# Residual and score carried in the gathered row: the second mixture's tiles scatter finished rows into the output

## What is computed

```python
def _L1_ffn_ref(hidden_states, w_red, wg, W1, b1, W2, b2):
    B, T, E, C, H, G = (2, 512, 8, 256, 512, 16)
    x = hidden_states.reshape(-1, c)
    x_red = x @ w_red
    wg_n = wg / jnp.maximum(jnp.linalg.norm(wg, axis=1, keepdims=True), 0.0001)
    logits = x_red @ wg_n.T
    gates = jax.nn.softmax(logits, axis=1)
    scores = jnp.max(gates, axis=1)
    idx = jnp.argmax(gates, axis=1)
    h = gelu(x @ W1[idx] + b1[idx])          # the expert that idx names
    o = h @ W2[idx] + b2[idx]
    o = o * scores[:, None]
x = x + _L1_ffn_ref(_layernorm(x, axis=-1), ...)
```

## Time and profile before

| | |
|---|---|
| median of 3 runs | 1151.25 us (1150.07 to 1156.2) |
| span of the profiled execution | 1143.9 us, first to last instruction |
| that execution's own time | not shown apart; the median is 7.35 us above its span |
| busy share of PE, DVE, ACT, POOL | 86%, 65%, 42%, 25% |
| last attention stage and routing | 912 to 1039 us |
| second mixture | 1039 to 1128 us |
| after it | 1128 to 1143.9 us |

### The profile page before, as it was taken

The page is one execution under the profiler, slowest core; times in us unless marked ns, Lnnn a source line. Parts: engine busy times, 40 slices in busy tenths (PEclk is TensorE's granted clock), DMA queues, the critical chain, the costliest instruction groups (busy, mean ns, idle before and its releaser), DMA issues.

```text
span 1143.9 us, 20648 instructions
## 1 busy us (share of the span) xinstructions
PE 982.2 (86%) x6905; PEld 591.4 (52%) x6905; DVE 742.5 (65%) x1952; ACT 478.9 (42%) x1055; POOL 280.5 (25%) x242
## 2 busy tenths in 40 slices
PE   7878789878898799999998876898899898987893
PEld 3555455546465488888885442333333333335662
DVE  3484677684878766666663476578777857545665
ACT  3443725342433344444442320446666657532331
POOL 0333524523320233444331001100010011112551
PEclk8999989998998899999999997669999988677997
DMA  8442020003535411111115486233163041231225
GB/s 289 150 129 110 2 74 1 19 1 93 142 98 166 146 49 53 49 53 48 48 40 164 96 152 126 54 42 53 43 112 75 2 131 61 87 126 37 79 76 176
DMA packets 69506, 98.64 MB, mean 86 GB/s; under 512 B 6528, under 2 KB 56960, under 8 KB 66976
## 3 DMA queue, kind: packets, MB, share of 16 engines
q1 hardware_dynamic: 60000, 63.75, 20.3%
q0 software_dynamic: 9408, 33.56, 11.0%
HBM read 70.10 MB, written 27.13 MB: 85 GB/s over the span
## 4 chain that ended last, share of the span: by engine, by line
PE 50%; DVE 28%; ACT 7%; DMA 7%; issue 4%; POOL 2%; SPq 1%; DVEq 0%; ACTq 0%; POOLq 0%
PE pb L1004 11%; PE pb L1021 7%; DVE MX L1943 5%; PE pb L1109 4%; PE pb L1022 3%; PE pb L769 3%; PE pb L1133 2%; PE pb L1087 2%; PE pb L848 2%; PE pb L838 2%; PE pb L792 2%; DMA xr<-rows,gi 2%; PE pb L1057 2%; ACT EX L1423 2%; DVE TQ L1552 1%
## 5 line engine op out<-in xcount | busy, mean ns | idle before, releaser
L1366 ACT ACTIVATE m<-pb,b1m 128x128 f32<-128x128 f32 x404 | 115.5, 369 | 172.0 <-PE pb L1004 169.8
L1423 ACT ACTIVATE EX<-pb 128x512 f32<-128x512 f32 x256 | 137.1, 599 | 115.7 <-PE pb L1133 114.9
L1943 DVE TENSOR_REDUCE MX<-pb 128x1 f32<-128x512 f32 x256 | 158.4, 683 | 41.0 <-PE pb L1087 40.8
L1004 PE MATMUL pb<-xt,w1h 128*128 128x128 f16 x1616 | 157.2, 221 | 3.8 <-issue 3.0
L1021 PE MATMUL pb<-w,mh 128*128 x404 | 149.4, 379 | 5.6 <-DVE ml L1854 5.2
L763 PE MATMUL pb<-identh 128*128 128x512 f16 x558 | 139.9, 408 | 15.5 <-DVE UZ L1588 8.8
L1004 PEld LDWEIGHTS pb<-xt,w1h 128*128 x1616 | 120.4, 99 | 42.0 <-issue 6.0
L1004 PE MATMUL pb<-xt,w1l 128*128 128x128 f16 x808 | 112.5, 220 | 0.0
L1022 PE MATMUL pb<-w,ml 128*128 x404 | 110.1, 273 | 0.0
L2155 POOL DMA_INDIRECT outs<-ob,di x62 | 61.3, 989 | 174.2 <-DVE ob L1869 174.2
L763 PEld LDWEIGHTS pb<-identh 128*128 128x128 f16 x558 | 55.9, 103 | 88.8 <-issue 21.4
(11 more groups left out here) (319 smaller groups left out, 1602.9 us busy)
## 6 DMA issues: line engine op xcount, KB each, us to landing
SR<-in_w1m SPq DMA_DIRECT2D x20, 512.0 KB, 5.6
SR<-in_w2m SPq DMA_DIRECT2D x14, 512.0 KB, 4.5
GB<-outs SPq DMA_DIRECT2D x12, 512.0 KB, 6.8
KS<-kd SPq DMA_DIRECT2D x48, 128.0 KB, 5.6
SRW<-in_w2m SPq DMA_DIRECT2D x10, 512.0 KB, 5.1
QS<-qd POOLq DMA_DIRECT2D x18, 256.0 KB, 10.1
kd<-KHL POOLq DMA_DIRECT2D x8, 512.0 KB, 5.7
vd<-VAB POOLq DMA_DIRECT2D x4, 1024.0 KB, 4.9
```

Source lines behind the costliest of these rows:

```text
L1004: ins = pe.matmul(k.ap[:, h4 * TOK:(h4 + 1) * TOK], wt[:, bass.ds(regs[j], 128)], M.xt[j % 2][:, xc, :], start=i == 0, stop=i == 5)
L1366: ins = act.activation(M.m32[x % 2][:, h4, :], k.ap[:, h4 * TOK:(h4 + 1) * TOK], M.func, bias=M.b1[:, bass.ds(reg + 4 * g + h4, 1)], scale ...
L1423: act.activation(EX[m % len(EX)][:, i, :], k.ap, ACT.Exp, scale=0.25).then_inc(k.out, 1)
L1943: v.tensor_reduce(mx[:, t, 2 * s + j:2 * s + j + 1], k.ap, AX.X, ALU.max).then_inc(k.out, 1)
```

## The change

A row of `rows1` becomes 2,056 bytes: the 1,024 bytes of the two float16 halves, then 256 float32 of the residual `X`, then the score and one zero. In each `gate(b)` SP writes the residual part when `XQ` is done, and the score part when DVE has made `scr` of this batch; for that the exponential of the gate values moves from the routing into each gate, on DVE (subtract, then reduce and reciprocal after `place`) and ACT (exponential). POOL's first gather waits for these writes also. In `experts(E1)` there are seven buffers `xr` in place of four, in the space that `GB1` had; the gather no longer waits for PE's transposes of the buffer's last tile. DVE makes a third operation on each `ob`: times the score plus the residual, both from `xr`. POOL scatters `ob` into the output itself, with a bounds check that leaves out slots whose target is beyond row 2,047. `finish` waits for the last three scatters only.

```diff
-                self.xr = [rings(f"xr{L}_{i}", 128, 2 * D, dt=F16) for i in range(4)]
+                width, dt = ((2 * D, F16), (2 * D + 2, F32))[L]
+                self.xr = [(rings, rest)[L](f"xr{L}_{i}", 128, width, dt=dt) for i in range((4, XR)[L])]
...
-                self.rows = nc.dram_tensor(f"rows{L}", (NT * P, 2 * D), F16, kind="Internal").ap()
-                self.outs = nc.dram_tensor(f"outs{L}", (2 * NT * P + n * TOK, D), F32, kind="Internal").ap()
+                self.rows = nc.dram_tensor(f"rows{L}", (NT * P, width), dt, kind="Internal").ap()
+                self.outs = (nc.dram_tensor("outs0", (2 * NT * P + n * TOK, D), F32, kind="Internal").ap() if L == 0
+                             else out.rearrange("b s d -> (b s) d"))
...
             def gate(b):
+                rows = E1.rows[b * S:b * S + S].rearrange("(t p) d -> p t d", p=128)
                 yield from pause(GAP)
+                w.wait_ge(sem("xg"), b + 1)
+                load("hx", rows[:, :, D:2 * D], X[:, 4 * b:4 * b + 4, :])
                 for n in (GAP, GAP, GAP + 1):
                     M.skip(1)
                     yield from pause(n)
...
                 for _ in range(2):
                     M.skip(1)
                     yield from pause(GAP)
+                w.wait_ge(sem("scr"), b + 1)
+                load("hs", rows[:, :, 2 * D:2 * D + 2], scr[:, 4 * b:4 * b + 4, :])
...
             def finish():
                 all_out(w, E1)
-                for b in range(NB):
-                    load(f"g{b}", GB1[b][:, :, :], E1.outs[b * S:b * S + S].rearrange("(t p) d -> p t d", p=128))
-                for t in range(3, NT, 4):
-                    w.wait_ge(sem("x4"), t // 4 + 1)
-                    load("out", ov[:, t - 3:t + 1, :], X[:, t - 3:t + 1, :])
-                w.wait_ge(sem("d_out"), n["out"])
...
+                w.wait_ge(sem("exz"), b + 1)
+                z = exz[:, 4 * b:4 * b + 4, :]
+                act.activation(z, z, ACT.Exp).then_inc(sem("ez"), 1)
...
+                    if L:
+                        x = M.xr[j % XR]
+                        w.wait_ge(*k.ev)
+                        w.wait_ge(*tile_dma("x", L, j))
+                        v.scalar_tensor_tensor(out=M.ob[j % 3][:, :], in0=M.ob[j % 3][:, :], scalar=x[:, 2 * D:2 * D + 1], in1=x[:, D:2 * D],
+                                               op0=ALU.mult, op1=ALU.add).then_inc(*c.up("done"))
...
                 place(R1, b, psum_m)
+                w.wait_ge(sem("ez"), b + 1)
+                v.tensor_reduce(scr[:, bt, 0], exz[:, bt, :], AX.X, ALU.add).then_inc(*c.up("v"))
+                w.wait_ge(*c.last)
+                v.reciprocal(scr[:, bt, 0], scr[:, bt, 0]).then_inc(*c.up("scr"))
...
                 def fetch(j):
-                    if j >= 4:
+                    if L == 0 and j >= 4:
                         w.wait_ge(*eX.take().mm)
...
                 def store(j):
-                    w.wait_ge(*eD.take().ev)
-                    pool.indirect_dma_start(out=M.outs, out_offset=bass.IndirectOffsetOnAxis(ap=r.di[:, j:j + 1].bitcast(U32), axis=0),
-                                            in_=M.ob[j % 3][:, :], in_offset=None).then_inc(tile_dma("o", L, j)[0], 16)
+                    w.wait_ge(*eD.take().ev if L == 0 else (sem("done"), j + 1))
+                    out_rows = bass.IndirectOffsetOnAxis(ap=r.di[:, j:j + 1].bitcast(U32), axis=0)
...
+                        pool.indirect_dma_start(out=M.outs, out_offset=out_rows, in_=M.ob[j % 3][:, :], in_offset=None,
+                                                bounds_check=NT * P - 1, oob_is_err=False).then_inc(tile_dma("o", L, j)[0], 16)
...
                 w.wait_ge(sem(f"d_hl{L}"), 16 * NB)
+                if L:
+                    w.wait_ge(sem("d_hx"), 16 * NB)
+                    w.wait_ge(sem("d_hs"), 16 * NB)
```

More of the change, by code:

```diff
@@ L237, in build, with __init__ @@
         class Experts:
-            def __init__(self, L, starts, hc, n, func, b1, b2, te, rings):
+            def __init__(self, L, starts, hc, n, func, b1, b2, te, rings, rest=None):
                 self.L, self.hc, self.n, self.func, self.b1, self.b2, self.te = L, hc, n, func, b1, b2, te
@@ L333, in build @@
         lgz1, top1, idxu1 = BZ("lgz1", 128, NT, E), BZ("top1", 128, NT, 8), BZ("idxu1", 128, NT, 8)
-        scr = BZ("scr", 128, NT)
+        scr = BZ("scr", 128, NT, 2)
         tei1 = [BZ(f"tei1_{i}", 1, N1) for i in range(3)]
@@ L348, in build @@
         b2m1 = EZ1("b2m1", 128, E * D)
-        E1 = Experts(1, [[o, o + 8 * K] for o in (MZ.start + 32 * K, MZ.start + 48 * K)] + [[MZ.start + 64 * K, last_zone]], 4, N1, ACT.Gelu, b1m1, b2m1, tei1, EZ1)
-        GB1 = [nc.alloc_sbuf_tensor_at(f"GB1_{i}", [128, 4, D], F32, offset=MZ.start + 4 * i * K) for i in range(NB)]
+        E1 = Experts(1, [[o, o + 8 * K] for o in (MZ.start + 32 * K, MZ.start + 48 * K)] + [[MZ.start + 64 * K, last_zone]], 4, N1, ACT.Gelu, b1m1, b2m1, tei1, EZ1,
+                     Zone(nc, MZ.start, 16 * K))
         PB = [ctx.enter_context(nc.psum_tensor(f"pb{i}", [128, 1024], F32)) for i in range(4)]
@@ L421, in tile_dma @@
         def tile_dma(what, L, j):
-            k = 4 if what == "x" else 3
-            return sem(f"d_e{what}{j % k}"), 16 * (j // k + 1 + (0, (N0 + k - 1 - j % k) // k)[L])
+            k = (4, XR)[L] if what == "x" else 3
+            return sem(f"d_e{what}{L}{j % k}"), 16 * (j // k + 1)
         def all_out(w, M):
@@ L1344, in route @@
                     act.activation(d01[:, :], d01[:, :], ACT.Exp).then_inc(sem("e01"), 1)
-                else:
-                    w.wait_ge(sem("exz"), 1)
-                    act.activation(exz[:, :, :], exz[:, :, :], ACT.Exp).then_inc(sem("ez"), 1)
             def experts(M):
@@ L1828, in route @@
                     v.tensor_tensor(ww[:, 1, :], d01[:, :], ww[:, 0, :], ALU.mult).then_inc(*c.up("ww"))
-                else:
-                    v.tensor_tensor(exz[:, :, :], lgz1[:, :, :], top1[:, :, 0:1].to_broadcast([128, NT, E]), ALU.subtract).then_inc(*c.up("exz"))
-                    w.wait_ge(sem("ez"), 1)
-                    v.tensor_reduce(scr[:, :], exz[:, :, :], AX.X, ALU.add).then_inc(*c.up("v"))
-                    w.wait_ge(*c.last)
-                    v.reciprocal(scr[:, :], scr[:, :]).then_inc(*c.up("scr"))
             def experts(M):
@@ L1993, in wg_norm @@
                 v.memset(R1.Mc[:, :], 0.0)
+                v.memset(scr[:, :, :], 0.0)
                 w.wait_ge(sem("d_we"), 3 * 16)
@@ L2033, in gate @@
                 w.wait_ge(*c.last)
+                bt = slice(4 * b, 4 * b + 4)
+                v.tensor_tensor(exz[:, bt, :], lgz1[:, bt, :], top1[:, bt, 0:1].to_broadcast([128, 4, E]), ALU.subtract).then_inc(*c.up("exz"))
                 for t in range(4 * b, 4 * b + 4):
@@ L2043, in gate @@
                 yield from pause(GAP)
-            def finish():
-                for t in range(NT):
-                    w.wait_ge(sem(f"d_g{t // 4}"), 48)
-                    ins = v.scalar_tensor_tensor(out=X[:, t, :], in0=GB1[t // 4][:, t % 4, :], scalar=scr[:, t:t + 1], in1=X[:, t, :], op0=ALU.mult, op1=ALU.add)
-                    if t % 4 == 3:
-                        ins.then_inc(*c.up("x4"))
             order(dict(start=start, kv_load=nop, loads1=nop, loads2=nop, pre=pre, s_exp=s_exp, rest=rest, mlp=mlp, kv=kv, split=split,
@@ L2146, in fetch @@
                 def fetch(j):
-                    if j >= 4:
+                    if L == 0 and j >= 4:
                         w.wait_ge(*eX.take().mm)
-                    pool.indirect_dma_start(out=M.xr[j % 4][:, :], out_offset=None, in_=M.rows,
+                    pool.indirect_dma_start(out=M.xr[j % len(M.xr)][:, :], out_offset=None, in_=M.rows,
                                             in_offset=bass.IndirectOffsetOnAxis(ap=r.gi[:, j:j + 1].bitcast(U32), axis=0)
```

14 lines of the change are left out of this document (10 added, 4 removed).

## The result

| | before | the change |
|---|---|---|
| first comparison | 1150.54 us (20 runs) | 1153.47 us (20 runs), ratio 1.0061 [1.0037, 1.0086] |
| second comparison | 1142.63 us (25 runs) | 1154.07 us (4 runs), ratio 1.0102 [1.0054, 1.0150] |

The change costs 0.4 to 0.9% by the first comparison and 0.5 to 1.5% by the second; 0.61% of 1150.54 is 7.0 us. The forecast was 2.1 us less, 1149.1. The median lies in its range, but the sign is wrong and the effect is 9 us off.

What follows compares the result with a forecast made beforehand. The prediction took the loop through POOL to bound the mixture, PE close behind. Tail -14.1, loop +7.6, start +1.9, gates +2.5 give -2.1 us against the median 1151.25: 1149.1 us, 8 in 10 between 1141.5 and 1158.5.

Steps and rivals of the forecast that it cites:

- What bounds the kernel: Last mixture: a loop through POOL, store to gather to PE to store, gives 3.5 us a tile; PE's own pace 3.13.
- The tail: End of the program: after the last scatter has landed nothing is left, so read-back and final operations go, -14.1 us.
- The bounds check: POOL's scatters: priced at nothing; between 0 and 0.2 us per store, it would cost up to 1.8 us.
- the final step isn't what it says: Rival, scatters: out-of-bounds slots cost POOL 0.5 us each, +4.8, total 1153.9 us; within the 0.50 shared with the forecast.
- The third operation and the wide gather: Mixture loop: per two tiles 0.46 us for DVE's operation plus 0.4 for the gather, less slack; +7.6 us.
- The rival in which the wide gather alone decides: Mixture loop: later gather landings, with a slow tiny write, make the kernel slower, about +6.5, 1157.8 us; chance 0.21.
- The sum of the loop: Last mixture: 11 x 0.46 + 10 x 0.4 = 9.1, less 0.15 for each of 10 gathers, +7.6 us.
- if the step is over 4.1: Sign in the mixture: a store step over 4.1 us means the gather's size was priced too low; 3.8 to 3.95 expected.
- The start: Start of the mixture: first gather waits for the last score write; +1.9 us, between +0.5 and +4.2.
- The rival by which tiny pieces are read, changed and written: Score writes: +4.2 at the start and +1.9 ahead of the weights, total +1.4, 1152.7 us; within the shared 0.50.
- The gates: Last attention stage: later weight loads +0.7, exponentials waiting for DVE +0.4 and +1.4; sum +2.5 us, between 0.5 and 6.
- within 0.5%: Whole kernel: forecast and near relatives (tiny pieces, slow scatter) all within 5.8 us of no change; chance 0.50.

## Why the prediction was wrong

**What bounds the kernel: right.** The loop through POOL was the bound of the mixture, with PE close behind. Opened by one tile, it gives PE's pace: 2.94 to 3.03 us a tile in three kernels, where I had read 3.13 off PE. One reading was wrong: the 4.1 and 2.2 us of the earlier trace rows are the same waits, seen by PE's weight loads and by its multiplies. They fall on 6 tiles and not on 9, and their sum is no number. Neither alone explains the step from 3.13 to 3.485; the nearness of 6.3 to it was chance.

**The tail: step failed.** "After the last scatter has landed nothing is left" was worth -14.1. Measured -8.7. The program ends 6.8 us after POOL's last instruction. In the kernel before POOL's last scatter was issued by 1128.33; 6.8 us behind that is 1135.1, beside the read-back and the final operations (worked out from the other traces, not seen in this one). Once these went, it was next. I had not asked what is late next after the longest chain.

**The bounds check: step failed.** "I give the bounds check on POOL nothing", at most 0.2 us. It is 0.57 us ahead of each scatter and 0.13 in it. POOL is in the loop, so it was 0.30 us a tile. From the first gather to the last store the change takes 104.9 us, the run with every slot inside its bound and no fall of the clock 103.0, and the one without the check 95.9: the check is 7.1. The rival "the final step isn't what it says" had 0.5 us a store and +4.8, the right size for the wrong reason: it laid it to the slots out of bounds, and the run with none of them costs the same.

**The third operation and the wide gather: right.** Priced together at 0.86 us for two tiles less slack, some 0.35 a tile. Measured 0.28 + 0.13 = 0.41: the operation was priced a little low and the gather a little high. The step between DVE's operations is 0.46, as taken from the earlier trace rows. From the first gather to the last store the kernel without the check takes 95.9 us and the kernel before 88.3, so the two cost 7.6 together, as forecast. Against the 103.0 of the run without a fall of the clock, the narrow gather saves 4.0 there and the missing operation 4.8. The rival in which the wide gather alone decides falls: it is 4 of 16.6 us.

**The clock: not in the sum.** I took PE to stay at full clock through the mixture. In the change it fell twice in the first six tiles, about 1.9 us.

**The sum of the loop.** Forecast +7.6 from the first gather to the last store; measured 1.75 + 13.1 + 1.8 = +16.6. Of the 9.0 that are missing, the check is 7.1 and the clock 1.9. The forecast's mark stands: "if the step is over 4.1" (it is 4.30, 4.16 in the steady part) a price was too low, but I named the gather's, and it was the check's.

**The start: about right.** +1.9 forecast, +1.5 measured: 0.3 for reduce and reciprocal, 1.2 for the write. Its 8-byte pieces were down 1.8 us after `scr`, near my fast end of 1.5 (forecast 2.6), and the gather followed 0.84 later, not 0.27. (The range's low end, +0.5, leaves out this 0.27; by its own terms it is +0.8.) The rival by which tiny pieces are read, changed and written was to bring them down after 4.9 us, and at that price it falls. The Trainium skill ("DMA: Bandwidth & Descriptors", opening table) states this for transfers under 512 B; the last score write, down after 1.8 us, shows no cost of that size. The median over the four score writes is 3.5 us, the same as for the four residual writes of 512 KB. What the small pieces cost beyond a write's fixed time no run isolates.

**The gates: not settled.** +2.5 forecast. From `md` to `sel` the changed kernel's traces have 119.2 to 122.1 us, the two with the gates as before 121.9 and 117.4. The spread of 3 to 4 us in this stage is larger than the term. That the weight loads come late was right; that it costs 0.7 was not seen.

All together: tail +5.4 and loop +9.0 against the forecast, start and gates -5.4 (of `md` to first gather, 4.4 forecast, -1.0 measured, a difference of two single traces and within their spread): 9.0 us, from -2.1 to +6.9. The chance for "within 0.5%" was 0.50 and for slower 0.21; the measured 0.61% lies just beyond that edge, on the side that I thought least likely.

## What to carry to other kernels

When a longest chain is cut off at the end of a program, price what ran beside it: here the last scatter and POOL's way out were a floor of 7.8 us under a tail of 16.5. An option on an instruction of the engine that closes the loop can be an operation of its own, to be bounded by the size of the operation itself (a scatter of 1 us) and not by nothing. And where three small additions all lie in one loop, first see whether the loop can be opened: one more tile of lead made 0.7 us a tile into 0.1, and turned a loss of 0.6% into a gain of 1.2%.

## What the runs showed of the hardware

- A bounds check on a scatter of 128 rows costs POOL 0.57 us ahead of it and 0.13 in its issue, whether slots are left out or not.
- The program with the change ends 6.8 us after POOL's last instruction, with no work to be seen, while 4.5 us more of PE or 2.9 of SP beside it change nothing. The profile lays this wait to PE.
- A gather of 128 rows of 2,056 bytes lands after 3.6 us by the median, one of 1,024 bytes after 2.8.
- TensorE's granted clock fell to its lower level inside the mixture, behind a wait of PE for a gather in an otherwise busy loop (0.67 on the average of 5 us). The traces with two such falls take 1.6 to 2.5 us longer from first gather to last store than the one with none. A wait as long (2.28 us) was followed by no fall there.
